# A five-stage tower on one core: the token mixer's parameters computed once, the zero fills spread over the turns, a bias moved between stages, and the second attention's weights in halves with a squared table root

## The chip, the cores and the metric

The kernel runs as one program on one core of a Trainium2 chip. Its time is the device time of one execution in microseconds (us); the median of several executions is compared. One execution was also taken by the hardware profiler, and all rows below come from that one.

## The reference

Sixteen sequences (B = 16) of 257 tokens (T, one class token and 256 others) of width 256 (D) pass through five blocks. All data are float32.

```
h = tok(log_dt, inv_A_real, A_imag, B_ri, x)     # V = exp(log_dA * arange(L)); K = 2 Re(einsum(C*B, V))
h = concat(cls_tok, h)                           # (16, 257, 256)
h = h + retention(layernorm(h))                  # 16 heads, decay mask, group norm, Wout
y = layernorm(h); z = layernorm(y)*g1 + b1
y = y + softmax_attention(z) @ Wp + bp           # causal, 16 heads
y = y + moe(layernorm(y)*g2 + b2)                # 8 experts, top 2
h = h + y
h = h + stablemax_attention(layernorm(h))        # s = 1/(1 - x(1 - x/2(1 - x/3))), x = logits - max
h = h + product_keys(rmsnorm, top 8 of 64 keys)  # gated by retrieved experts
```

The token mixer needs dA = (1 + dtA/2)/(1 - dtA/2) with dt = exp(log_dt), A = -exp(inv_A_real) + i A_imag, and powers of dA. In the second attention all x are at most 0, so a weight is the reciprocal of a cubic in x.

## The kernel before

`tower` calls the stages one after the other; each opens a `Room` with its own buffers and semaphores, and closes with a barrier of all engines. Intermediate tensors go through HBM scratch. Every engine's order is written out by hand, and semaphores set who waits for whom; an engine runs its own list strictly in order. There is no planner.

**token_mixer** (L152) treats 128 pairs of channels in four turns of 32 (PC). For a turn SP loads six pieces of parameters (`load`, L188 to L194). VectorE then runs a chain in `turn`: an exponential by series, the division, and eight squarings E of dA (L258 to L291), 55 operations on tiles of 128 x 32, each of which waits for the one before (`chain.link`); then the powers V and weighted inputs W by doubling (L293 to L315), on tiles of up to 128 x 1024. TensorE multiplies V and W, ScalarE copies out (L225), and SP stores in eight transfers (L203). The engines run the turns in loops (`Fori`); VectorE's and TensorE's have two turns in a pass. V and W have two buffers, and the tile E one.

**retention** (L505) goes over sequences in turns with three overlapping stages: A forms q, k and v of the next sequence, B scores and weighs the present one, C normalises the one before. A turn has 16 steps. SP loads one sequence a turn (L567) and stores in four transfers (L573). ScalarE copies K, V and the results from PSUM. Before its turns ScalarE issues 16 transfers (`FILLS`) of a zero tile of 128 x 4592 floats, 2.3 MB each, into `ys` (L695), rows that the experts' stage uses much later; the stage waits for them at its end. All constants, the decay table of 3.1 MB last, are waited for before the first matmul.

**enter_attention** (L1378) goes over eight groups of 512 tokens and a tail of 16: a projection by TensorE (L1428), h1 = h + projection (L1453), two layer norms in `first`, `second`, `third` on VectorE, transposes (L386), and three stores a group in ScalarE's queue: the transposed x (L1511), hx = h1 + x (L1514) and x (L1515). `first(g+1)` waits until the rows of an earlier group, which use the same buffers, are stored.

**experts** (L1544) starts with a router: for each group of 512 tokens TensorE runs `project` (four tiles of two products with `wp`, L1678, and one product of a row of ones with the bias, L1679), `ranks` of the group before last (per tile a pair of 8-column products, L1702 and L1703), and `gates` (transposes L386, then L1693). VectorE adds the projection to x and to hx (`enter`), picks experts (`choose`), normalises (`leave`) and places (`settle`); POOL scatters rows (L2013). SP's loads of a group wait until two groups before are projected and normalised. 40 tiles of expert work follow.

**attention** (L846) is called twice: causal (softmax), then not causal (stablemax). Its first part projects all sequences and finds the row maxima. The second goes over sequences (a batch) in STEPS = 16 places; the tables `SCORE_AT`, `SUMS_AT` and `VALUE_AT` say at which place an engine does which unit. Not causal, a batch has eight steps v, each for four heads and half of the keys: TensorE forms four 128 x 257 scores in PSUM (L1056), ScalarE squares them (`weigh`, L1193), VectorE makes the cubic (`cubic`, L1311) and frees the scores, and ScalarE takes the reciprocal as exp(-ln) (`log` L1200, `exponential` L1204, each over 128 x 1028). The scores have one set of PSUM banks. For each four heads (two steps) `products` (L1087, L1088), `copy_sums` (L1320), `spread_sums` (L1127), the reciprocal of the sums (L1211, L1218) and `end` (L1327) follow. One table set (`LOG_SET`) is loaded ahead.

## Time and profile before

| what | value |
|---|---|
| median of 3 runs | 4756.81 us (4755.84 to 4758.91) |
| profiled execution | 4754.65 us, its span 4752.8 us |
| granted clock of TensorE, mean | 0.871 |
| token mixer | 0 to 215 us |
| retention | 266 to 622 us |
| entry of attention | 622 to 762 us |
| first attention (causal) | 762 to 1310 us |
| experts, router first (to about 1530) | 1310 to 2294 us |
| second attention, its second part from 2626 | 2294 to 3182 us |
| product keys | 3182 to 4753 us |
| TensorE, VectorE, ScalarE, POOL busy over all | 80%, 52%, 33%, 7% |

Busy times are shares of the span; a stage's start and end are times from the first instruction. PE is TensorE, PEld its weight loads, DVE VectorE, ACT ScalarE, SP the engine that issues most transfers; a q behind an engine's name means its sequencer. Float32 matmuls appear as two instructions each. What stands after `<-` behind an idle time is what ended it. The granted clock is 1.0 at the upper level (2.4 GHz) and 0.5 at the lower (1.2 GHz); a value between them is a mean over a stretch.

### The profile page before, as it was taken

How to read it: one execution, taken by the hardware profiler on the slowest of the kernel's cores; microseconds unless marked ns; L12 is line 12 of the kernel's file. 1: busy time of each engine (PE TensorE's matmuls, PEld its weight loads, DVE VectorE, ACT ScalarE, POOL GpSimd, SP SyncE). 2: the span in 40 equal slices, each digit the busy share in tenths (PEclk: the TensorE clock that was granted, in tenths of full speed). 3: DMA queues.
4: the chain of work that ended last, by engine and by line, in shares of the span. 5: the costliest groups of instructions: out<-in, count | busy, mean ns of one | idle time of the engine just before them, and what ended most of it. 6: DMA issues, size and time to landing. Idle time of an engine off the chain costs nothing. (4 is left out here: it accounts for less than half of the span.)

```text
span 4752.8 us, 94621 instructions
## 1 busy us (share of the span) xinstructions
PE 3820.0 (80%) x38224; PEld 2748.7 (58%) x38224; DVE 2451.1 (52%) x6959; ACT 1567.9 (33%) x2605; POOL 326.3 (7%) x451
## 2 busy tenths in 40 slices
PE   1249946998886899993688777765999999999999
PEld 1236634656554777773344333334877777787776
DVE  8626654542234000003456344427887888888881
ACT  0013312225500323221221788852333333333331
POOL 0011111000024000004100000000000000000000
PEclk8569968999955999996789777866999999999997
DMA  1282142001133545443200000020000000000000
GB/s 33 55 349 83 25 134 78 20 21 32 26 105 104 202 167 186 166 179 120 73 15 15 14 15 18 16 90 28 9 9 15 9 9 15 9 9 15 9 5 5
DMA packets 162688, 295.59 MB, mean 62 GB/s; under 512 B 36688, under 2 KB 138944, under 8 KB 154480
## 3 DMA queue, kind: packets, MB, share of 16 engines
q1 hardware_dynamic: 122720, 199.73, 13.7%
q10 hardware_dynamic: 33296, 73.37, 4.0%
q0 software_dynamic: 6272, 16.85, 1.1%
q8 instruction: 288, 4.72, 0.4%
q14 instruction: 112, 0.92, 0.1%
HBM read 184.17 MB, written 105.20 MB: 61 GB/s over the span
## 5 line engine op out<-in xcount | busy, mean ns | idle before, releaser
L2272 PE MATMUL peer_total<-peer_up,peer_hid 128*128 128x256 f32 (+1 forms) x2112 | 566.0, 395 | 0.0
L2250 PE MATMUL peer_work<-peer_xnT,peer_down 128*128 128x256 f32 (+1 forms) x2176 | 558.4, 380 | 0.0
L2250 PEld LDWEIGHTS peer_work<-peer_xnT,peer_down 128*128 128x128 f32 x2176 | 410.6, 196 | 74.1 <-ACT peer_hid L2303 21.4
L2303 ACT ACTIVATE peer_hid<-peer_work 128x256 f32<-128x256 f32 (+1 forms) x544 | 202.6, 372 | 710.6 <-PE peer_work L2250 710.6
L2272 PEld LDWEIGHTS peer_total<-peer_up,peer_hid 128*128 128x128 f32 (+1 forms) x2112 | 376.5, 187 | 66.8 <-issue 15.3
L2323 ACT ACTIVATE peer_G<-peer_scat 128x512 f32<-128x512 f32 x258 | 272.3, 1056 | 261.5 <-PE peer_scat L2210 261.5
L2421 DVE TENSOR_TENSOR peer_hid<-peer_hid,peer_G 128x256 f32<-128x256 f32 (+1 forms) x544 | 216.3, 407 | 272.1 <-ACT peer_hid L2303 264.1
L1960 DVE TENSOR_TENSOR moe_yb<-moe_bank,moe_w 128x512 f32<-128x512 f32 x40 | 27.7, 692 | 624.1 <-PE moe_bank L1750 624.1
L2210 PEld LDWEIGHTS peer_scat<-peer_one_j,peer_one_i 64*64 64x64 f32 x16448 | 275.3, 138 | 123.2 <-issue 123.0
L1738 PE MATMUL moe_bank<-moe_xgT,moe_w 128*128 128x256 f32 x1280 | 295.2, 384 | 52.0 <-ACT moe_mid L1817 45.7
L2210 PE MATMUL peer_scat<-peer_one_j,peer_one_i 64*64 64x32 f32 x16448 | 302.6, 223 | 36.5 <-DVE peer_one_j L2400 14.6
L1738 PEld LDWEIGHTS moe_bank<-moe_xgT,moe_w 128*128 128x128 f32 x1280 | 230.2, 191 | 105.7 <-ACT moe_mid L1817 61.0
L1750 PE MATMUL moe_bank<-moe_w,moe_mid 128*128 128x256 f32 x1280 | 282.6, 379 | 0.0
L1311 DVE SCALAR_TENSOR_TENSOR stable_U<-stable_U,stable_bank 128x1028 f32<-128x1028 f32 x128 | 156.7, 1224 | 215.6 <-ACT stable_U L1193 215.6
L1750 PEld LDWEIGHTS moe_bank<-moe_w,moe_mid 128*128 128x128 f32 x1280 | 243.2, 190 | 33.1
L1260 DVE TENSOR_REDUCE stable_negmax<-stable_bank 128x2 f32<-128x514 f32 x256 | 168.5, 688 | 125.1 <-PE stable_bank L998 125.1
L1056 PE MATMUL stable_bank<-stable_QT,stable_KT 32*128 32x257 f32 x1024 | 118.5, 531 | 138.9 <-DVEq L1313 138.3
L998 PE MATMUL stable_bank<-stable_KT,stable_QT 32*128 32x257 f32 x1024 | 167.0, 448 | 33.1 <-DVE stable_negmax L1260 32.6
L1817 ACT ACTIVATE moe_mid<-moe_bank,moe_w 128x256 f32<-128x256 f32 x320 | 147.6, 475 | 127.3 <-PE moe_bank L1738 127.3
L1056 PEld LDWEIGHTS stable_bank<-stable_QT,stable_KT 32*128 32x128 f32 x1024 | 54.1, 228 | 201.3 <-issue 201.3
L338 PE MATMUL tok_acc<-tok_V,tok_W 64*64 64x64 f32 x1024 | 37.6, 243 | 165.2 <-DVE tok_prod L316 165.2
L2400 DVE TENSOR_TENSOR peer_one_j<-peer_eq,peer_FT 128x1024 f32<-128x1024 f32 x129 | 158.0, 1225 | 4.4
(361 smaller groups left out, 6320.7 us busy)
## 6 DMA issues: line engine op xcount, KB each, us to landing
moe_w<-in_moe_w SPq DMA_DIRECT2D x40, 2180.0 KB, 8.7
ys<-ret_zeros ACTq DMA_DIRECT2D x16, 2296.0 KB, 52.5
moe_xg<-xs SPq DMA_DIRECT2D x40, 256.0 KB, 8.7
ys<-moe_yb ACTq DMA_DIRECT2D x40, 256.0 KB, 9.0
soft_xT<-xT SPq DMA_DIRECT2D x32, 257.0 KB, 2.8
stable_xT<-xT SPq DMA_DIRECT2D x32, 257.0 KB, 2.8
ret_xT<-xT SPq DMA_DIRECT2D x16, 257.0 KB, 2.8
aT<-ret_cN SPq DMA_DIRECT2D x64, 64.2 KB, 2.1
```

Of the source, the lines that this page charges most:

```text
L998: last = mm(out[:, x, 0:T], QT[rows, b, hg, k * P:k * P + P], KT[rows, b, hg, :], start=True, stop=True)
L1056: last = mm(S[:, j, 0:T], KT[rows, g, hg, k * P:k * P + P], QT[rows, g, hg, :], start=True, stop=True)
L1260: last = v_.tensor_reduce(negmax[:, b % 2, k, at:at + 2], src[:, :, 0:T], AX.X, ALU.max, negate=True)
L1738: last = mm(hid[u % 2], w[:, s, at:at + P], xgT[:, k % 2, c, :], start=c == 0, stop=c == DC - 1)
L1750: last = mm(y[k % 2][:, j, :], mid[:, k % 2, hb, j * P:j * P + P], w[:, s, at:at + D], start=hb == 0, stop=hb == HB - 1)
L2210: last = mm(scat[64 * par:64 * par + 64, half, k * JB:k * JB + JB], one_i[part, s % 2, part_no * SUB // 2 + k, :], one_j[part, s % 2, part ...
L2250: last = mm(work[:, jj % 2, 0:nb], down[:, c, jj, :], xnT[:, g % 3, c, 0:nb], start=c == 0, stop=c == DC - 1)
L2272: last = mm(total[:b_rows, j, :], hid[:, e % NHID, j * P:j * P + b_rows], up[:, e, :], start=e == 0 and j == 0, stop=e == JB - 1, skip_gro ...
L2303: A(hid[:, jj % NHID, 0:nb], work[:, jj % 2, 0:nb], ACT.Gelu).then_inc(gelu_ready, 1)
L2323: A(to, scat[:, 0:halves, 0:SUB // 2 * JB].rearrange("p h (t j) -> p h t j", j=JB), ACT.Copy).then_inc(scat_taken, 1)
L2400: v.tensor_tensor(one_j[:q, s % 2], eq[:q, s % 2], wide(2, NKEYS), ALU.mult).then_inc(one_ready, 1)
L2421: v.tensor_tensor(hid[:, jj % NHID, 0:nb], hid[:, jj % NHID, 0:nb], G[:, g % 2, jj, 0:nb], ALU.mult)\
```

## The change

Five parts:

- token_mixer: parameters of all 128 pairs are loaded at once, and the chain up to the squarings E runs once on tiles of 128 x 128. The turns keep V, W and the products, take slices of E (`mine`), and are written out without loops. The class token is moved behind the parameter loads; B and C, which the turns alone use, have their own semaphore.
- retention: ScalarE issues one fill in each turn that has a stage B, at step 4, instead of 16 ahead of the turns.
- enter_attention and experts: the bias of the projection (`bp`) is added to x by VectorE in the entry stage (`xb`, L1465's neighbour), before hx and the stores; the router's bias products are dropped.
- experts: the ranks of a group are one pair of 32-column products instead of four pairs of 8 columns.
- attention, not causal: scores, square and cubic go in halves of two heads, each with its own signals; the reciprocal is the square of a table function 1/sqrt|x| (`Abs_reciprocal_sqrt`, the set `TABLE_SET[False]`), whose root ScalarE does (`root`) and whose square VectorE does in place (`weigh`), two steps later. Sums and the odd query take both root and square on ScalarE. Sums and values move to other places of the batch. The causal call keeps its operations and places.

```diff
-        tmp = r.sb("tmp", [P, 6, PC])
-        E = r.sb("E", [P, 2, 8, PC])
...
+        tmp = r.sb("tmp", [P, 6, PAIRS])
+        E = r.sb("E", [P, 2, 8, PAIRS])
...
-            def load(t):
-                sp.wait_ge(inputs_free, t + 1)
-                at = bass.ds(t * PC, PC)
-                for h2 in range(2):
-                    half = slice(64 * h2, 64 * h2 + 64)
-                    sp.dma_start(par[half, 0, :], log_dt[h2:h2 + 1, at].broadcast_to([64, PC])).then_inc(loaded, 16)
-                sp.dma_start(par[:, 1, :], inv_A_real[:, at]).then_inc(loaded, 16)
-                sp.dma_start(par[:, 2, :], A_imag[:, at]).then_inc(loaded, 16)
-                sp.dma_start(par[:, 3:5, :], B_ri[:, :, at]).then_inc(loaded, 16)
-                sp.dma_start(c_ri[:, :, :, :], C_ri[:, :, at, :]).then_inc(loaded, 16)
+            for h2 in range(2):
+                half = slice(64 * h2, 64 * h2 + 64)
+                sp.dma_start(par[half, 0, :], log_dt[h2:h2 + 1, :].broadcast_to([64, PAIRS])).then_inc(loaded, 16)
+            sp.dma_start(par[:, 1, :], inv_A_real).then_inc(loaded, 16)
+            sp.dma_start(par[:, 2, :], A_imag).then_inc(loaded, 16)
+            sp.dma_start(par[:, 3:5, :], B_ri).then_inc(weights_in, 16)
+            sp.dma_start(c_ri[:, :, :, :], C_ri).then_inc(weights_in, 16)
...
+            a, b, den, x2, y2, na = (tmp[:, k, :] for k in range(6))
+
+
+            dve.wait_ge(loaded, 64)
+            x, k_, rem, p, dt = par[:, 0, :], tmp[:, 0, :], tmp[:, 1, :], tmp[:, 2, :], ex[:, 0, :]
+            link(v.tensor_scalar(k_, x, 1.0 / LN2, None, ALU.mult))
...
+                mine = slice(t * PC, t * PC + PC)
 
                 dve.wait_ge(products_done, t + 1)
-                link(v.tensor_tensor(E[:, 0, 0, :], x2, den, ALU.mult))
...
+                    e = [E[:, c, k, mine].rearrange("p (a b) -> p a b", b=1).broadcast_to([P, PC, n]) for c in range(2)]
                     q = products(chain, [V[:, c, :, 0:n] for c in range(2)], e[0], e[1], PC * n)
                     v.tensor_tensor(V[:, 0, :, n:2 * n], q[0], q[1], ALU.subtract)
                     link(v.tensor_tensor(V[:, 1, :, n:2 * n], q[2], q[3], ALU.add))
...
+                if t == 0:
+                    dve.wait_ge(weights_in, 32)
+                bb = [par[:, 3 + c, mine].rearrange("p (a b) -> p a b", b=1).broadcast_to([P, PC, B]) for c in range(2)]
...
-                v.memset(prod[:, :, 0:1], 0.0).then_inc(inputs_free, 1)
-                dve.wait_ge(inputs_free, t + 2)
...
-            for k in range(FILLS):
-                act.dma_start(blank[:, k, :], zeros[:, :]).then_inc(filled, 16)
...
+                    if "B" in stages and s == SLOTS:
+                        act.dma_start(blank[:, bass.ds(g, 1), :].rearrange("p o n -> p (o n)"), zeros[:, :]).then_inc(filled, 16)
...
-LOG_SET = "natural_log_exp_and_others"
+TABLE_SET = {True: "natural_log_exp_and_others", False: "abs_reciprocal_sqrt_and_small"}
...
-SUMS_AT = {True: {3: 0, 7: 1, 11: 2, 15: 3}, False: {6: 0, 10: 1, 14: 2, 18: 3}}
+SUMS_AT = {True: {3: 0, 7: 1, 11: 2, 15: 3}, False: {8: 0, 12: 1, 16: 2, 20: 3}}
 SPREAD_LAG, END_LAG = 2, 3
-VALUE_AT = {1: "v0", 4: "v1", 6: "v_odd", 10: "odd_score"}
+VALUE_AT = {True: {1: "v0", 4: "v1", 6: "v_odd", 10: "odd_score"}, False: {5: "v0", 7: "v1", 9: "v_odd", 11: "odd_score"}}
...
+                if not causal:
+                    for x in range(2):
+                        if n:
+                            pe.wait_ge(s_taken, 2 * n + x - 1)
+                            stand()
+                        for j in range(2 * x, 2 * x + 2):
+                            rows = slice(SLOT * j, SLOT * j + SLOT)
+                            last = mm(S[:, j, 0:T], KT[rows, g, hg, k * P:k * P + P], QT[rows, g, hg, :], start=True, stop=True)
+                        last.then_inc(s_ready, 1)
+                    return
...
-                A(w_odd[:, g % 2, :], u_odd[:, :], ACT.Ln, scale=-1.0).then_inc(ln_odd_ready, 1)
+                A(w_odd[:, g % 2, :], u_odd[:, :], ACT.Abs_reciprocal_sqrt).then_inc(ln_odd_ready, 1)
                 act.wait_ge(ln_odd_ready, g + 1)
-                A(w_odd[:, g % 2, :], w_odd[:, g % 2, :], ACT.Exp, scale=-1.0).then_inc(w_odd_ready, 1)
+                A(w_odd[:, g % 2, :], w_odd[:, g % 2, :], ACT.Square).then_inc(w_odd_ready, 1)
...
+            def square(n, x):
+                act.wait_ge(s_ready, 2 * n + x + 1)
+                if n >= 2:
+                    act.wait_ge(ln_ready, n - 1)
+                A(U[:, n % 2, 2 * x:2 * x + 2, :], S[:, 2 * x:2 * x + 2, 0:T], ACT.Square, scale=-SCALE, bias=bend[:, :])\
+                    .then_inc(y_ready, 1)
+
+            def root(n):
+                act.wait_ge(t_ready, 2 * n + 2)
                 if n >= nw:
                     act.wait_ge(av_done, (n - nw) // 2 + 1)
-                A(W[:, n % nw, :, :], U[:, n % 2, :, :], ACT.Ln, scale=-1.0).then_inc(ln_ready, 1)
-
-            def exponential(n):
-                act.wait_ge(ln_ready, n + 1)
-                A(W[:, n % nw, :, :], W[:, n % nw, :, :], ACT.Exp, scale=-1.0).then_inc(w_ready, 1)
+                A(W[:, n % nw, :, :], U[:, n % 2, :, :], ACT.Abs_reciprocal_sqrt).then_inc(ln_ready, 1)
...
-                A(logs[:, n % 2, :], spread_out[:, 0:T], ACT.Ln).then_inc(log_ready, 1)
+                A(logs[:, n % 2, :], spread_out[:, 0:T], ACT.Ln if causal else ACT.Abs_reciprocal_sqrt).then_inc(log_ready, 1)
...
+                            n = g * SU + v
+                            square(n, 0)
+                            square(n, 1)
+                            if n:
+                                root(n - 1)
...
-                u = U[:, n % 2, :, :]
-                dve.wait_ge(y_ready, n + 1)
-                v_.scalar_tensor_tensor(u, u, REST, S[:, :, 0:T], ALU.add, ALU.mult).then_inc(t_ready, 1)
-                dve.wait_ge(t_ready, n + 1)
-                dve.sem_inc(s_taken, 1)
+                for x in range(2):
+                    u = U[:, n % 2, 2 * x:2 * x + 2, :]
+                    dve.wait_ge(y_ready, 2 * n + x + 1)
+                    v_.scalar_tensor_tensor(u, u, REST, S[:, 2 * x:2 * x + 2, 0:T], ALU.add, ALU.mult).then_inc(t_ready, 1)
+                    dve.wait_ge(t_ready, 2 * n + x + 1)
+                    dve.sem_inc(s_taken, 1)
+
+            def weigh(n):
+                w = W[:, n % nw, :, :]
+                dve.wait_ge(ln_ready, n + 1)
+                v_.tensor_tensor(w, w, w, ALU.mult).then_inc(w_ready, 1)
...
+                        n = g * SU + SCORE_AT[causal][s]
                         cubic(g, SCORE_AT[causal][s])
+                        if n >= 2:
+                            weigh(n - 2)
+                    if not causal and g == B and s == 0:
+                        weigh(B * SU - 2)
+                        weigh(B * SU - 1)
...
+            sp.dma_start(next_b[:, :], next_b_in.broadcast_to([P, D])).then_inc(const_in, 16)
...
-                v.tensor_tensor(hx[:rows, q, 0:tiles, :], h1[:rows, q, 0:tiles, :], x[:rows, q, 0:tiles, :], ALU.add)\
+                bias = next_b[:rows, :].rearrange("p (a d) -> p a d", a=1).broadcast_to([rows, tiles, D])
+                chain.link(v.tensor_tensor(xb[:rows, q, 0:tiles, :], x[:rows, q, 0:tiles, :], bias, ALU.add))
+                v.tensor_tensor(hx[:rows, q, 0:tiles, :], h1[:rows, q, 0:tiles, :], xb[:rows, q, 0:tiles, :], ALU.add)\
                     .then_inc(rows_ready, 1)
...
-                act.dma_start(tokens(x_out, t0, tiles, rows), x[:rows, q, 0:tiles, :]).then_inc(rows_stored[q], 16)
+                act.dma_start(tokens(x_out, t0, tiles, rows), xb[:rows, q, 0:tiles, :]).then_inc(rows_stored[q], 16)
...
-                        mm(proj[q][:rows, j, :], aT[:, q, c, j * P:j * P + rows], wp[:, c, :], start=c == 0, stop=False)
-                    last = mm(proj[q][:rows, j, :], ones[0:1, :rows], bp[0:1, :], start=False, stop=True)
+                        last = mm(proj[q][:rows, j, :], aT[:, q, c, j * P:j * P + rows], wp[:, c, :], start=c == 0, stop=c == DC - 1)
...
-                for j in range(tiles):
-                    mm(rank[:rows, j, :], before[:rows, :rows], both[:rows, g % 2, j, :], start=True, stop=False)
-                    last = mm(rank[:rows, j, :], ones[:, :rows], seen[:, g % 2, j, :], start=False, stop=True)
-                last.then_inc(rank_ready, 1)
+                n, flat = tiles * EXPERTS, "p j e -> p (j e)"
+                mm(rank_row[:rows, 0:n], before[:rows, :rows], both[:rows, g % 2, 0:tiles, :].rearrange(flat), start=True, stop=False)
+                mm(rank_row[:rows, 0:n], ones[:, :rows], seen[:, g % 2, 0:tiles, :].rearrange(flat), start=False, stop=True)\
+                    .then_inc(rank_ready, 1)
```

## Rows read from the trace of the kernel before

**Rows 1.** Windows of VectorE, token mixer: length, busy (instructions), granted clock, DMA share, GB/s.
```profile
10.10:22.95 12.85, 10.63 (x55) 1.00 0.00 1
...
22.95:54.95 32.00, 31.08 (x58) 1.00 0.08 19
...
147.70:160.40 12.70, 10.71 (x56) 0.89 0.03 5
```

**Rows 2.** Timeline, token mixer: start us, duration us, engine, line; idle before.
```profile
0.75 0.40 SPq L180 DMA_DIRECT2D tok_cls<-in_cls_tok  x1
...
2.81 1.21 SPq L190 DMA_DIRECT2D tok_par<-in_log_dt  x2
...
10.15 0.18 DVE L258 TENSOR_SCALAR tok_tmp<-tok_par 128x32 f32<-128x32 f32 x1 [9.27 <-DMA tok_c_ri<-in_C_ri]
...
25.29 0.29 DVE L243 TENSOR_TENSOR tok_prod<-tok_V,tok_E 128x128 f32<-128x128 f32 x1
...
102.89 0.18 DVE L258 TENSOR_SCALAR tok_tmp<-tok_par 128x32 f32<-128x32 f32 x1 [3.33 <-issue]
```

**Rows 3.** Timeline, retention's start.
```profile
288.38 1.92 PE L600 MATMUL ret_misc_a<-ret_xT,ret_wk 128*128 128x257 f32 x4
...
314.49 0.39 ACT L716 ACTIVATE ret_KT<-ret_misc_a 128x257 f32<-128x257 f32 x1 [51.06 <-issue]
...
321.94 17.84 SPq L567 DMA_DIRECT2D ret_xT<-xT  x2
...
400.24 0.41 SPq L567 DMA_DIRECT2D ret_xT<-xT  x1
```

**Rows 4.** DMA issues: engine, count, KB each, median us to landing.
```profile
tok_par<-in_A_imag SPq DMA_DIRECT2D x4, 16.0 KB, 1.8
...
ret_decay<-in_decay SPq DMA_DIRECT2D x1, 3088.0 KB, 14.6
...
moe_acc<-hx SPq DMA_DIRECT2D x8, 512.0 KB, 7.1
```

**Rows 5.** Timeline of VectorE, entry of attention.
```profile
689.56 1.22 DVE L1453 TENSOR_TENSOR mid_h<-mid_h,mid_out 128x1024 f32<-128x1024 f32 x1 [4.85 <-DMA x<-mid_x]
...
704.11 1.22 DVE L1453 TENSOR_TENSOR mid_h<-mid_h,mid_out 128x1024 f32<-128x1024 f32 x1 [4.61 <-DMA x<-mid_x]
```

**Rows 6.** Timeline of TensorE, router, and one projection of the entry stage.
```profile
1377.63 2.05 PE L1678 MATMUL moe_bank<-moe_wp,moe_aT 128*128 128x256 f32 x4
...
1379.62 1.22 PE L1679 MATMUL moe_bank<-moe_bp,moe_ones 1*128 1x256 f32 x2
...
1390.22 0.60 PE L1702 MATMUL moe_bank<-moe_both,moe_before 128*128 128x8 f32 x2
...
1393.66 1.95 PE L386 MATMUL moe_bank<-moe_ident,moe_xn 128*128 128x128 f32 x8
...
681.73 4.25 PE L1428 MATMUL mid_out<-mid_wout,mid_cT 128*128 128x256 f32 x16
```

**Rows 7.** Windows, all engines (PE, PEld, DVE, ACT, POOL): six router steps, two batches.
```profile
1354.85:1492.50 137.65, 128.42 (x385) 90.46 (x386) 59.09 (x276) 9.92 (x18) 45.47 (x47) 0.50 0.30 98
...
2700.30:2734.40 34.10, 24.63 (x181) 11.75 (x183) 14.42 (x20) 30.08 (x39) 1.41 (x2) 0.85 0.08 16
...
2734.40:2768.50 34.10, 26.87 (x155) 12.19 (x148) 13.83 (x20) 26.27 (x32) 1.41 (x2) 0.70 0.08 17
```

**Rows 8.** Groups of instructions: count, busy us, mean ns, idle before.
```profile
L1311 DVE SCALAR_TENSOR_TENSOR stable_U<-stable_U,stable_bank 128x1028 f32<-128x1028 f32 x128 | 156.7, 1224 | 215.6 <-ACT stable_U L1193 215.6
...
L1193 ACT ACTIVATE stable_U<-stable_bank,stable_bend 128x1028 f32<-128x1028 f32 x128 | 141.1, 1102 | 12.7 <-PE stable_bank L1056 12.6
...
L1960 DVE TENSOR_TENSOR moe_yb<-moe_bank,moe_w 128x512 f32<-128x512 f32 x40 | 27.7, 692 | 624.1 <-PE moe_bank L1750 624.1
...
L1145 ACT ACT_TABLE_LOAD x2 | 2.6, 1283 | 9.0 <-PEq L74 9.0
```

**Rows 9.** Timeline of VectorE, second attention: a copy behind a cubic.
```profile
2833.20 0.42 DVE L1320 COPY stable_OT<-stable_bank 128x257 f32<-128x257 f32 x1 [0.22 <-DVE stable_U L1311]
```

More of the change, by code:

```diff
@@ L201, in store @@
                         p0 = 64 * h2 + B * a
-                        dst = h_out[:, bass.ds(1 + h2 + t * (2 * PC), PC, 2), L1 * a:L1 * a + L1]
+                        first = 1 + h2 + t * (2 * PC)
+                        dst = h_out[:, first:first + 2 * PC - 1:2, L1 * a:L1 * a + L1]
                         sp.dma_start(dst, res[p0:p0 + B, :, :]).then_inc(stored, 16)
-            load(0)
-            with sp.Fori(0, turns - 1) as t:
-                load(t + 1)
+            sp.dma_start(cls[:, :], cls_tok[0:1, :].broadcast_to([B, D])).then_inc(cls_in, 16)
+            sp.wait_ge(cls_in, 16)
+            sp.dma_start(h_out[:, 0, :], cls[:, :]).then_inc(cls_out, 16)
+            for t in range(turns):
                 store(t)
-            store(turns - 1)
             sp.wait_ge(stored, 16 * 8 * turns + 16)
@@ L225, in copy_out @@
                 nc.scalar.activation(res[:, :, :], acc[:, :, :], ACT.Copy, scale=2.0).then_inc(res_ready, 1)
-            exponential(0)
-            with act.Fori(0, turns - 1) as t:
-                exponential(t + 1)
+            for t in range(turns):
                 copy_out(t)
-            copy_out(turns - 1)
         @block.vector
         def _(dve):
-            nc.vector.memset(prod[:, :, 0:1], 0.0).then_inc(inputs_free, 1)
             v = nc.vector
+            chain = Chain(dve, chained)
+            link = chain.link
             def products(chain, x, er, ei, n):
@@ new lines, in _ @@
+            link(v.scalar_tensor_tensor(rem, k_, -LN2_HI, x, ALU.mult, ALU.add))
+            link(v.scalar_tensor_tensor(rem, k_, -LN2_LO, rem, ALU.mult, ALU.add))
+            link(v.tensor_scalar(p, rem, 1.0 / math.factorial(EXP_TERMS), None, ALU.mult))
+            for n in range(EXP_TERMS - 1, 0, -1):
+                link(v.scalar_tensor_tensor(p, p, 1.0 / math.factorial(n), rem, ALU.add, ALU.mult))
+            link(v.tensor_scalar(two_k[:, :], k_, 127.0, float(1 << 23), ALU.add, ALU.mult))
@@ L317, in turn @@
                 dve.wait_ge(powers_ready, t + 1)
-                chain.done()
-            with dve.Fori(0, turns // 2) as n:
-                turn(2 * n, 0)
-                turn(2 * n + 1, 1)
+            for t in range(turns):
+                turn(t, t % 2)
         @block.tensor
@@ L340, in turn @@
                 last.then_inc(products_done, 1)
-            with pe.Fori(0, turns // 2) as n:
-                turn(2 * n, 0)
-                turn(2 * n + 1, 1)
+            for t in range(turns):
+                turn(t, t % 2)
 def groups(engine, step):
@@ L1217, in invert @@
                     act.wait_ge(ended, n - 1)
-                A(inv[:, n % 2, :], logs[:, n % 2, :], ACT.Exp, scale=-1.0).then_inc(inv_ready, 1)
+                if causal:
+                    A(inv[:, n % 2, :], logs[:, n % 2, :], ACT.Exp, scale=-1.0).then_inc(inv_ready, 1)
+                else:
+                    A(inv[:, n % 2, :], logs[:, n % 2, :], ACT.Square).then_inc(inv_ready, 1)
             odd_score(0)
```

169 lines of the change are left out of this document (70 added, 99 removed).

## The prediction

> **What bounds the kernel now.** The kernel is a row of stages with a barrier behind each, so a stage's gain is the kernel's gain, and each part is read in its own stage. I read the busy time by windows first, to see the stages; then the timeline of one period of each touched stage; then the waits that end last there. The executed time is 4754.65 us (span 4752.8 us, 1.85 us around it); the median of three runs, 4756.81 us, is 2.16 us more, so I work against 4754.65 and add 2.2 at the end. A change within 0.2% (9.5 us) couldn't be told from none.
>
> The token mixer is one VectorE chain. Each of its four turns begins with 55 small dependent operations, 12.85 us in the first and 12.70 us in the last, and goes on with 32 us of long ones; of the 12.85 VectorE is busy 10.63, so a link of width 32 takes 0.19 and a 0.04 us wait [rows 1]. Before it, VectorE stands 9.27 us until the largest parameter load is in, and between the two passes of its loop 3.33 us for "issue" [rows 2].
>
> Retention begins badly: ScalarE idles 51.06 us in "issue" before its first copy, because the sixteen fills of 2.3 MB stand ahead of it in its own order; TensorE has the first K projection done 24 us earlier [rows 3]. The entry of attention is held by a store: VectorE waits 4.85 us of a period of 704.11 - 689.56 = 14.5 us for a landing [rows 5].
>
> The experts' router is TensorE's: in 137.65 us TensorE is busy 128.42, at a granted clock of 0.50, the lower of its two levels (1.2 GHz) [rows 7]. In the second attention, a batch of eight steps takes 34.1 us with ScalarE busy 26 to 30 us, and TensorE at the lower level for part of it (0.70 to 0.85) [rows 7].
>
> **Token mixer.** The 55 links are done once at width 128 instead of four times at width 32. A 128-wide operation took 0.29 us [rows 2]; with the 0.04 wait 55 make 18. Removed: 12.85 + 2 x 12.75 + 12.70 = 51. Gain 33. Bounds: 12.8 if width were free, 23 if a link cost half as much again as that row: 28 to 38. The loop's 3.33 us goes with the loop. At the start four loads are waited for and not six, and the class-token load, its wait and its store no longer stand ahead: the first issue stays at 0.75, the fourth follows 1.9 later (0.6 each, from the pair at 2.81), and A_imag takes 1.8 to land, so VectorE starts at 4.5 and not 10.15, gain 5.6 [rows 2, 4]. The big load, now 2 MB, is needed only after the chain and the first V products, some 35 us on; four times the old one fits there. Later loads disappear from SP's queue, stores stay. VectorE's 32 us per turn, TensorE's products and the last stores stay as they are. The wait for products moves ahead of V only, and the products of two turns back are long done. Sum -42 (-36 to -47).
>
> **Retention.** The fills go into the turns, one per turn. ScalarE can then copy K as soon as TensorE has it: 290.3 (288.38 + 1.92) instead of 314.49, gain 24.2. The constants wait ends with the decay table, 3.1 MB in 14.6 us beside the fills [rows 4]; shared evenly with them it would be half alone, 7 less; I take 5.5 (bounds 0 to 8). Further, the early x loads lie behind the fills: from the issue at 321.94 to that at 400.24 four turns take 78.3 us, where the first of them shows 17.46 (17.84 for two issues less the second's own 0.4) [rows 3]; 78.3 - 69.8 = 8.5 us late, which goes too. On ScalarE one fill per turn costs its issue; it also queues ahead of that turn's four stores and x load. A fill is 2.3 MB, and by the decay row's rate lands in about 11 us, inside a 17.5 us turn. TensorE bounds these turns and ScalarE has slack, so I charge 0.2 us per turn, 3 in all (0 to 12). The last fill starts a turn and a half before the end. Sum -24 - 5.5 - 8.5 + 3 = -35 (-24 to -40).
>
> **Entry of attention.** The added bias addition is a 128x1024 tensor_tensor, 1.22 us as the one in the rows, in each of eight groups. It falls into VectorE's 4.85 us of waiting for a landing; the rows stored in that period were made one period earlier, so their store starts no later [rows 5]. So it is hidden; without the cover it costs 8 x 1.25 + 0.4. One more constant in SP's queue delays the first loads by 0.4 to 1. I take +1 (0 to +11).
>
> **Router.** Each tile's two wp products (2.05) are followed by a one-row bias product; from the first wp product to the first rank product a projection takes 1390.22 - 1377.63 = 12.6 us. Without the bias it is 16 matmuls in a row of the same shape, which the entry stage shows: 4.25 us. The router's own four in 2.05 would be 8.2 for sixteen, so the clock there was at the upper level for a good part [rows 6]. I take 5.5, nearer to the row of the same sequence, since here each projection starts at the lower level; 8.2 is the other bound. Ranks go from four pairs to one: 1393.66 - 1390.22 = 3.4 us to a quarter, 0.9, gain 2.5. The step of 137.65 / 6 = 22.9 becomes 13.3. What comes next: POOL's scatters take 45.47 / 6 = 7.6 us busy in a step and some issue gaps, VectorE has 59.09 / 6 = 9.8 [rows 7], loads land in 7.1 us [rows 4], all inside 13.3. Six steps give 57.6; the first two projections, back to back, 2 x 7.1 = 14; the last two ranks, half hidden by VectorE, 3. Sum -74. With 8.2 per projection: 6 x 6.9 + 9 + 3 = -53. With 4.25, and transposes and gates at the upper level too, a step of 11.4: -91.
>
> **Second attention.** ScalarE loses one of three passes of about 1.1 us per step and splits the square: with 1.1 for a pass and up to 0.35 for the second start, 30.1 - 8 x 1.05 + 8 x 0.35 = 24.5 us per batch at most [rows 7, 8]. VectorE gets that work: eight products of width 1028 (1.22 each, as the cubic of that width) = 9.8; eight split cubics, 2 x 0.69 for 1.22 (0.69 from the 512-wide row), = 1.3 [rows 8]; and after each of 16 halves the 0.22 us hand-over that the copy shows, 3.5 [rows 9]. With 14.4 busy now: 29.0. VectorE becomes the bound: no batch can be under 29.0. Its new wait, for ScalarE's root, is for the root of two steps back, which ScalarE did after the squares of the step before, so it is over when VectorE comes to it. What else is on the path: the weighted products wait for VectorE's square, which comes 1.2 us after the cubic; while TensorE stands there, nothing behind it starts, the next scores included. TensorE's busy time is 24.63 at 0.85 and 26.87 at 0.70 [rows 7], by that slope 22.4 at the upper level and 29.9 at the lower; four waits of 0.9 make 26 and 33.5. So a batch is 29 us at the upper and 33.5 at the lower level; with the share of the lower one as in these two batches (mean 0.78, so 45%) 31. Sixteen batches: 16 x (34.1 - 31) = 50, less 1 for a longer tail: -49. Bounds: -82 (29 throughout), 0 (34.1, TensorE's order binding). In halves the scores of one half run beside the cubic of the other, which takes the old wait of TensorE for VectorE away; that is the reason why VectorE can be kept full.
>
> In this stage one table load stands at the start and none follows, though Square, Identity, Ln and Exp alternate: two loads for two attentions, 1283 ns each [rows 8]. The Trainium skill, page "ScalarE: Activation LUTs", section "Table sets: the hidden batching unit", names relu, copy, identity and abs as filler of every set; Square and the new root are not in that list, and section "What ACT_TABLE_LOAD costs" prices a switch at 2.66 us. If the square needed another set, the rule speaks against the change; that is rival D, worked out from the rows. No row here shows the new set. By the page's price its loads would cost 384 x 2.66 = 1021 us of ScalarE.
>
> **Sum.** -42 - 35 + 1 - 74 - 49 = -199: 4754.65 - 199 + 2.2 = 4558.
>
> **Rivals.** A, the clock takes the second attention's gain: with TensorE at the lower level most of the time, the wait for the squared root replaces the wait for the cubic, batches stay at 34, and the time is 4607. For it: the clock already falls to 0.70 there, and TensorE's gaps remain; against it: less waiting per step means a denser TensorE. B, everything at its better bound: 29 per batch and the router at 11.4: 4558 - 33 - 17 = 4508. For it: the entry stage's rise within one projection. C, the fills do not leave the path: if each fill issued in a turn holds ScalarE as long as the early ones did (51.06 / 16 = 3.2 us), retention gains nothing, 4593. Against: those filled the queue, one per turn doesn't. D, slower: the table of the new set lacks Square. Then each step switches to the root and back, and sums twice per group: up to 24 loads per batch at 1.28 = 30.8 us; ScalarE's batch is 24.5 + 30.8 = 55.3, and 16 x 21.2 = 339 us are lost against 150 won elsewhere: 4946. It ends slower than before from 15 loads per batch on. Against: the old set held Square beside two transcendentals.
>
> **Chances.** Forecast (4530 to 4585) 0.52, A 0.20, B 0.16, C 0.08, D 0.04. The parts don't depend on one another, so a shortfall in one doesn't turn the sign: faster 0.95, same 0.01, slower 0.04. The range reaches from B to a little beyond A: 4502 to 4630.
>
> **What would show it.** Token mixer: 55 links once, its stage over near 173 of the span (215 now). Retention: ScalarE's first K copy within 1 us of its projection, turns of 17.5 from the first. Router: no 1-row matmuls, step 12 to 14.5, granted clock above 0.50. Second attention: one table load, VectorE busy over 75%, batches of 29 to 33. The forecast is wrong if batches stay at 34, if the router's step stays above 15, or if any stage not touched moves.

## The result, and the profile after

The changed kernel takes 4567.23 us, the median of four runs (4555.41 to 4583.38), against 4757.86 of the kernel before on the same chip (4755.84 to 4763.22). The ratio is 0.960, its 95% interval 0.957 to 0.963. The forecast was 4558. The profiled execution took 4574.35 us, 180.3 less than the one before; its stages, from the first instruction to the last (transfers left out):

| stage | before | after | start to start, change | forecast |
|---|---|---|---|---|
| token mixer | 203.9 | 157.7 | -42.5 (with its start) | -42 |
| entry of retention (untouched) | 48.1 | 48.6 | +0.5 | 0 |
| retention | 351.1 | 317.5 | -33.6 | -35 |
| entry of attention | 135.4 | 138.1 | +2.9 | +1 |
| first attention (untouched) | 543.6 | 545.6 | +2.0 | 0 |
| experts with the router | 980.0 | 900.9 | -79.1 | -74 |
| second attention | 882.5 | 849.6 | -32.8 | -49 |
| last stage (untouched) | 1567.9 | 1570.2 | +2.3 | 0 |

The token mixer's first two times begin at different points, a short memset at 0.82 us before and the first link at 4.81 after, so its change is read from the start of the next stage.

Token mixer: the window of VectorE from its first instruction to the end of the chain (length, busy and instructions, granted clock, DMA share, GB/s). It answers to the first line of [rows 1]: 18.15 us once in place of four times 12.7 or more. It begins at 4.81 instead of 10.15 [rows 2].
```profile
4.81:22.96 18.15, 16.29 (x55) 1.00 0.30 113
```

Retention: the timeline around the first K copy. ScalarE follows the projection of 242.33 at once, with no "issue" in front of it as in [rows 3].
```profile
242.33 1.63 PE L588 MATMUL ret_misc_a<-ret_xT,ret_wk 128*128 128x257 f32 x4
...
244.06 0.39 ACT L704 ACTIVATE ret_KT<-ret_misc_a 128x257 f32<-128x257 f32 x1 [22.63 <-PE ret_misc_a L588]
```
Its DMA issues (count, KB each, median us to landing): a fill lands in 9.9 us, where the page of before has 52.5, and the decay table in 10.3 instead of 14.6 [rows 4].
```profile
ys<-ret_zeros ACTq DMA_DIRECT2D x16, 2296.0 KB, 9.9
...
ret_decay<-in_decay SPq DMA_DIRECT2D x1, 3088.0 KB, 10.3
```

Entry of attention, VectorE: the new addition stands at L1478, and the wait for the landing, 4.85 in [rows 5], is 3.60: the cover paid for it. The period stays at 617.19 - 602.64 = 14.55 us.
```profile
602.64 1.22 DVE L1465 TENSOR_TENSOR mid_h<-mid_h,mid_out 128x1024 f32<-128x1024 f32 x1 [3.60 <-DMA x<-mid_xb]
611.14 1.23 DVE L1478 TENSOR_TENSOR mid_xb<-mid_x,mid_next_b 128x1024 f32<-128x1024 f32 x1
...
617.19 1.22 DVE L1465 TENSOR_TENSOR mid_h<-mid_h,mid_out 128x1024 f32<-128x1024 f32 x1 [3.57 <-DMA x<-mid_xb]
```

Router, timeline of TensorE, answering to [rows 6]: sixteen products in 5.27 us, one pair of rank products instead of four, and ahead of the next projection a new wait, for a load.
```profile
1281.42 5.27 PE L1692 MATMUL moe_bank<-moe_wp,moe_aT 128*128 128x256 f32 x16 [0.70 <-DMA moe_acc<-hx]
1286.53 0.30 PE L1715 MATMUL moe_bank<-moe_both,moe_before 128*128 128x32 f32 x2
1286.67 0.39 PE L1716 MATMUL moe_bank<-moe_seen,moe_ones 128*128 128x32 f32 x2
...
1296.60 0.80 PE L1692 MATMUL moe_bank<-moe_wp,moe_aT 128*128 128x256 f32 x1 [5.14 <-DMA moe_acc<-hx]
```

Windows over all engines (PE, PEld, DVE, ACT, POOL busy, then granted clock, DMA share, GB/s), answering to [rows 7]: six router steps; the second part of the second attention, from its first square to its end; and two neighbouring stretches of it, one at each level of the clock.
```profile
1270.21:1344.61 74.40, 54.24 (x265) 46.21 (x265) 56.78 (x269) 9.92 (x18) 44.42 (x45) 0.77 0.54 179
2478.83:2994.77 515.94, 453.23 (x2596) 218.63 (x2596) 396.93 (x572) 342.79 (x558) 21.17 (x29) 0.73 0.08 15
2680.64:2694.30 13.66, 11.49 (x88) 5.48 (x86) 12.25 (x19) 11.30 (x21) 1.42 (x2) 1.00 0.21 40
2694.30:2711.37 17.07, 16.37 (x76) 7.77 (x76) 12.45 (x18) 9.24 (x14) 0.00 (x0) 0.50 0.00 0
```
The same part of before:
```profile
2628.08:3177.34 549.26, 406.44 (x2595) 183.19 (x2593) 229.46 (x316) 451.85 (x558) 20.98 (x29) 0.78 0.07 14
```
The router's step is 74.4 / 6 = 12.4 us. In the second attention ScalarE's load went to VectorE (229 to 397 us busy), and the part lost 33.3 us. In these two stretches VectorE is busy 12.25 of 13.66 us at the upper level, TensorE 16.37 of 17.07 at the lower: a different engine is nearly full in each. I counted the 127 steps by the granted clock at their middle: 68 at the upper level with 3.32 us on average, 59 at the lower with 4.67; before, 78 with 3.94 and 49 with 4.71. The lower level holds 54% of the time instead of 44%. These means are no price of the clock, because they hold different kinds of steps: after the change v = 0, 1 and 2 fall at the lower level in 45 of 48 cases, v = 4, 5 and 6 at the upper level in 45 of 48. By kind, v = 5 fell from 6.5 us to 3.5, and v = 2 rose from 4.1 to 7.2 and v = 0 from 4.1 to 5.1, since products, sums and values were moved to other places.

The long step v = 2 (7.19 us) in TensorE's timeline, at the lower level: products, odd products and a value unit, 5.2 us, all ahead of the next scores.
```profile
2673.37 1.94 PE L1081 MATMUL stable_bank<-stable_W,stable_V 128*32 128x257 f32 x16
2675.24 1.22 PE L1082 MATMUL stable_bank<-stable_w_odd,stable_V_odd 16*128 16x257 f32 x2
2676.39 2.07 PE L1111 MATMUL stable_bank<-stable_wv,stable_xT 128*128 128x256 f32 x4
2678.39 1.24 PE L1046 MATMUL stable_bank<-stable_QT,stable_KT 32*128 32x257 f32 x8
```
Groups of the second attention, as in [rows 8]: VectorE's halves of 0.69 us, its square, and still two table loads for two attentions.
```profile
L1309 DVE SCALAR_TENSOR_TENSOR stable_U<-stable_U,stable_bank 128x514 f32<-128x514 f32 x256 | 176.5, 690 | 64.4 <-ACT stable_U L1188 44.8
...
L1316 DVE TENSOR_TENSOR stable_W<-stable_W 128x1028 f32<-128x1028 f32 x128 | 157.2, 1229 | 18.8 <-DVE stable_U L1309 0.5
...
L1139 ACT ACT_TABLE_LOAD x2 | 2.6, 1283 | 9.3 <-PEq L74 9.3
```
VectorE's two halves in its timeline, 1.53 us together:
```profile
2687.51 1.53 DVE L1309 SCALAR_TENSOR_TENSOR stable_U<-stable_U,stable_bank 128x514 f32<-128x514 f32 x2
```

### The profile page after: what moved, and what is told of

It reads as the page before. It is cut to its first block and busy times, and to the rows that moved or that the text cites. A ratio compares the mean times of both kernels' runs of the same rounds, so it can differ in the third digit from the quotient of the medians.

```text
span 4572.5 us, 94477 instructions
## 1 busy us (share of the span) xinstructions
PE 3759.8 (82%) x38062; PEld 2721.0 (60%) x38062; DVE 2602.4 (57%) x7054; ACT 1458.2 (32%) x2602; POOL 326.6 (7%) x451
## 5 line engine op out<-in xcount | busy, mean ns | idle before, releaser
L1188 ACT ACTIVATE stable_U<-stable_bank,stable_bend 128x514 f32<-128x514 f32 x256 | 164.9, 681 | 156.4 <-PE stable_bank L1046 152.6
L1309 DVE SCALAR_TENSOR_TENSOR stable_U<-stable_U,stable_bank 128x514 f32<-128x514 f32 x256 | 176.5, 690 | 64.4 <-ACT stable_U L1188 44.8
L1046 PE MATMUL stable_bank<-stable_QT,stable_KT 32*128 32x257 f32 x1024 | 182.2, 550 | 19.6 <-DVEq L1311 17.5
L986 PE MATMUL stable_bank<-stable_KT,stable_QT 32*128 32x257 f32 x1024 | 167.6, 449 | 32.8 <-DVE stable_negmax L1257 32.4
L1316 DVE TENSOR_TENSOR stable_W<-stable_W 128x1028 f32<-128x1028 f32 x128 | 157.2, 1229 | 18.8 <-DVE stable_U L1309 0.5
```

What stands on the lines that cost most here:

```text
L986: last = mm(out[:, x, 0:T], QT[rows, b, hg, k * P:k * P + P], KT[rows, b, hg, :], start=True, stop=True)
L1046: last = mm(S[:, j, 0:T], KT[rows, g, hg, k * P:k * P + P], QT[rows, g, hg, :], start=True, stop=True)
L1309: v_.scalar_tensor_tensor(u, u, REST, S[:, 2 * x:2 * x + 2, 0:T], ALU.add, ALU.mult).then_inc(t_ready, 1)
```

## Experiments

Theory: the gain is a sum over stages, and in the second attention it is cut by TensorE at its lower level. Rivals: VectorE or the root sets the batch and the clock is a bystander; or the halves are the gain. Barriers keep the stages apart, so one kernel can carry an edit in several. "Part" is the second attention from its first square to its end, "batch" eight steps of it (the mean of the first fifteen batches), "lower share" the share of the time from the first square to the last at the lower level; single executions unless a range is given. The same part was profiled in three executions, the changed kernel twice and once in the kernel before (below): 515.9, 520.4 and 515.3 us. So a difference of some 5 us between two kernels says nothing.

**Unused products of 128 rows, and of 32.** Behind the scores of v = 6, 7, 0 and 1, into PSUM columns that nobody reads:
```
+ free = O[((s - 2) // 4) % 2]
+ for x in range(1):     # at s in (1, 3, 13, 15); 128 -> 32 in the second kernel
+     mm(free[:, 258:512], spread[0:128, :], KT[0:128, g, x % HG, 0:254], start=True, stop=True)
```
Where the expectations, here and below, speak of eight products a batch, two in each place, the kernels have one in each place: four a batch, 60 in all, which the trace records as two instructions each (2716 instead of 2596).

> The changed kernel with eight unused products per batch of the second attention (two 128-row products of 254 columns in each of four steps that have only 32-row scores: behind v = 6, 7, 0 and 1). In the changed kernel a step takes 3.32 us while the granted clock is at the upper level and 4.67 at the lower, and the lower one holds 54% of the time. Theory (TensorE at the lower level sets the step there, and the clock falls where TensorE has little but 32-row scores): the lower share falls under 0.35, batches from 31.5 to 27.5 to 29.5, second part of the stage from 516 to 445 to 480 us, whole kernel 4500 to 4540. Rival (VectorE or the root sets the step, the clock is a bystander): the share may move, the batch stays at 31.5 or more, the part at 516 or more. Second rival (the clock doesn't answer to it): share 0.54, and eight products of about 0.5 us make the batch 2 to 4 us longer.

> The same eight unused products per batch in the same places, with 32 rows in place of 128. Theory (what TensorE does in those steps decides its clock, and 32-row products don't raise it): the lower share stays near 0.54 or grows, the batch is 31.5 to 35 us. Rival (any product that fills the gap does it): share and batch as with 128 rows.

Windows of the part, 128 rows and then 32:
```profile
2474.83:2954.49 479.66, 409.46 (x2716) 198.82 (x2716) 392.50 (x572) 338.41 (x558) 21.10 (x29) 0.91 0.08 16
```
```profile
2490.55:3021.38 530.83, 482.50 (x2716) 253.19 (x2716) 396.86 (x572) 342.45 (x558) 21.14 (x29) 0.72 0.07 15
```
The same 60 additional products made the part 36 us shorter with 128 rows (lower share 0.16, batch 29.1) and 15 us longer with 32 (share 0.56, batch 32.5); the kernels took 4535.38 and 4600.11 us, all as expected. VectorE's work is the same in both. So the clock is no bystander, and between these two kernels it went with the rows of the products.

With 128 rows five batches ran at 1.00 throughout; one of them, and one of the changed kernel for comparison:
```profile
2652.53:2680.63 28.10, 24.02 (x175) 11.70 (x172) 24.52 (x37) 21.13 (x37) 1.42 (x2) 1.00 0.10 20
```
```profile
2664.61:2696.66 32.05, 29.18 (x166) 14.30 (x166) 25.07 (x37) 21.51 (x35) 1.42 (x2) 0.71 0.09 18
```

**Three parts undone, one per stage.**
```
router:     + mm(proj, ones[0:1, :rows], bp[0:1, :], start=False, stop=True)   # entry as before
retention:  + for k in range(FILLS): act.dma_start(blank[:, k, :], zeros)      # ahead of the turns
attention:  - square(n, 0); square(n, 1)      + square(n)     # cubic and scores in full width too
```


> The changed kernel with one part undone in each of three stages, which barriers keep apart: the one-row bias products back in the router (and the entry stage as before), the sixteen fills ahead of retention's turns, the second attention in full width with the new root and VectorE's square. Expected: router's projection back from 5.5 to about 12.6 us, its step from 12.4 to 19 to 21, clock at 0.50; retention from 317.5 to about 351; entry of attention from 138 to 135.4. Second attention, theory (halves keep VectorE and TensorE beside each other): scores, square and cubic follow one another again, batches of 33 to 35. Rival (the pass taken from ScalarE is the gain, halves do nothing): 31 to 32.

Windows of five router steps and of the part, and the router's timeline:
```profile
1313.47:1415.45 101.98, 94.29 (x262) 62.68 (x262) 49.15 (x230) 8.26 (x15) 36.52 (x37) 0.50 0.36 119
2566.88:3092.49 525.61, 417.95 (x2596) 195.83 (x2596) 378.09 (x444) 323.77 (x430) 21.14 (x29) 0.72 0.07 15
```
```profile
1313.47 2.05 PE L1682 MATMUL moe_bank<-moe_wp,moe_aT 128*128 128x256 f32 x4
1315.45 1.22 PE L1683 MATMUL moe_bank<-moe_bp,moe_ones 1*128 1x256 f32 x2
```
Projection 12.59, step 20.4 us, all at 0.50; the experts stage is 962.2. Retention is 350.4 us, the entry 134.9: as expected. The second attention lost only 9.7 us (batch 32.3), or 5 against the longest execution with halves: between the two expectations, nearer to the rival that the halves do little.

**Three other edits.**
```
router:     mm(proj, ident[:, :rows], bp[:, :], ...)     # 128 rows instead of 1, same sum; entry as before
retention:  8 fills ahead; then one half fill per turn
attention:  - v_.tensor_tensor(w, w, w, ALU.mult)   + A(W, W, ACT.Square)   # halves and root kept
```


> The changed kernel with three other edits in three stages. Router: the same bias products with 128 rows (identity by a bias row on every partition) in place of one row. Theory (one-row products hold the clock down): projection 6.5 to 8 us, step 12.5 to 14.5, clock well above 0.50; rival (their time alone counted): projection 12.6, step 19 to 21, clock 0.50. Retention: eight fills ahead, the rest in half fills, one per turn. Theory (a full DMA queue held ScalarE): ScalarE's first K copy within 1 us of its projection, stage 318 to 325; rival (the fills' share of the DMA engines): copy still 10 us or more late, stage 330 or more. Second attention: halves and new root, the square on ScalarE as a third pass. Theory (ScalarE was the bound before and is so again, 21 + 8 x 1.06 = 30 us busy per batch): 32 to 35; rival (VectorE's new square is the present bound): under 31.

Windows, router's timeline, and DMA issues (count, KB each, us to landing):
```profile
1282.64:1350.00 67.36, 58.08 (x261) 50.93 (x262) 48.57 (x230) 8.25 (x15) 35.61 (x36) 0.75 0.55 180
2493.85:3012.89 519.04, 468.69 (x2596) 224.62 (x2596) 249.38 (x444) 455.22 (x686) 21.08 (x29) 0.70 0.07 15
```
```profile
1286.47 0.59 PE L1696 MATMUL moe_bank<-moe_bp,moe_ident 128*128 128x256 f32 x2
1286.91 1.03 PE L1695 MATMUL moe_bank<-moe_wp,moe_aT 128*128 128x256 f32 x4
```
```profile
ret_decay<-in_decay SPq DMA_DIRECT2D x1, 3088.0 KB, 14.8
ys<-ret_zeros ACTq DMA_DIRECT2D x8, 2296.0 KB, 33.0
```
Router: the same number of products as with one-row bias, at 0.75 instead of 0.50; projection 6.9 to 7.5, step 67.36 / 5 = 13.5 us. Of the 10.5 us that the change took off a step, the ranks are 2.5 (22.9 to 20.4), the clock that came with the one-row products 6.9 (20.4 to 13.5), and the rest 1.1 (13.5 to 12.4): the bias products' own time, less the wait for the rows' load, which grew from 0.3 us a step to 1.8. Retention: the K copy follows its projection at once (249.57, projection from 247.62), yet the stage is 328.9 us, 11.4 more than with fills in turns and longer than expected: the shared DMA engines cost that. The decay table lands 4.5 us later, and the next two loads of x take 15.2 and 16.1 us instead of 2.6. The other 21.5 (350.4 - 328.9) are for the most part ScalarE held by its queue: from the first projection to the first product with the decay table 38.1 us pass with sixteen fills ahead, 17.8 with eight. Second attention: batch 32.0, at the low end of what was expected; but the part, 519.0, lies within the three executions with VectorE's square (515.3 to 520.4), so at this clock that square brought nothing that can be seen.

So at this clock neither undoing the halves nor undoing VectorE's square gives back much of the 33.3 us. Both kernels keep the later places of the root, the sums and the values: in the kernel before, ScalarE took the logarithm in the same step as the cubic that it waits for, and now it takes the root one step later. What these places alone bring, no run separates.

**The second attention's part alone, in the kernel before.**

> The kernel before with nothing but the second attention's part of the change. Theory (stages are kept apart by barriers, gains add up): stage 849 to 852 us from start to end against 882 before and 850 with all parts, all other stages as before within 3 us, whole kernel 4720 to 4728. Rival (a stage's clock depends on what ran before it): the stage differs by over 10 us from the 850.

848.8 us, 0.2 below the expected range, and 4717.76 in all, 2.2 below; all other stages within 1.4 us of before. The gains add up over stages.

**Value products moved, without and with unused products.**
```
- False: {5: "v0", 7: "v1", 9: "v_odd", 11: "odd_score"}
+ False: {7: "v0", 11: "v1", 14: "v_odd", 15: "odd_score"}     # the odd query's weights at s = 1
```


> The changed kernel with the value products of the second attention moved behind the scores of the odd steps (v0 behind v = 3, v1 behind 5, the odd ones behind 7), where no weighted products stand; no unused products. Theory (at either level the next scores wait on TensorE behind products and a value unit in one step): the long step v = 2 falls from 7.19 to 5 us, the even steps to 3.3 at the upper level, batch 29 to 31. Rival (VectorE sets the step, TensorE's order is no matter): batch 31.5, the time only moves between steps. What the clock does with the new order is open; were it to stay low for longer, the batch could be 32 or more.

> The same move, and four unused 128-row products per batch, behind the scores of v = 1 and v = 7. Theory (both the order and the clock count): lower share under 0.25, batch 27 to 28.5, second part of the stage 435 to 460 us, whole kernel 4490 to 4520. Rival (with the clock up, VectorE is the bound whatever TensorE's order): 29, as with the eight unused products alone.

Both missed: batches of 34.0 and 32.0, 4609.0 and 4574.69 us. The steps v = 0 and v = 2 did fall, from 5.12 to 2.86 and from 7.19 to 4.98; but v = 7 rose to 9.57, because the odd score now stood right behind the odd values and waited for VectorE's copy of them (2.80 us) and then took 3.58 us (1.90 at the upper level in the changed kernel), the next scores behind it:
```profile
2709.90 3.58 PE L1104 MATMUL stable_bank<-stable_QT,stable_K_odd 128*16 128x257 f32 x8 [2.80 <-DVE stable_v_odd L1301]
2713.41 1.24 PE L1046 MATMUL stable_bank<-stable_QT,stable_KT 32*128 32x257 f32 x8
```
A wait that I had added myself stands in these two; the mended move below, with the same number of unused products, takes it out.

**The changed kernel again, the unused products timed, and the move mended** (odd values one step earlier; one, two and one unused products at s = 1, 3, 15):
```
+ False: {7: "v0", 11: "v1", 13: "v_odd", 15: "odd_score"}
```


> The changed kernel once more, for its spread: 4555 to 4584 us, ratio to before 0.957 to 0.963. Theory (the second attention's time follows the share of the lower clock, which differs from run to run): times fall with the mean granted clock of the run; rival: no relation.

> The changed kernel with the eight unused 128-row products, timed: 4525 to 4545 us, below every run of the changed kernel by over 10 us, if the clock in the second attention is what its lower batches came from; 4555 or more in some runs if the first look was a lucky phase.

> As the move with four unused products, but the odd rows' value product behind v = 6 and their score behind v = 7, one step apart, so that TensorE doesn't stand behind the copy between them (2.80 us of waiting and a step of 9.57 in the run with the move alone). Theory (that wait was all that the move lost): no step above 4.5 us, batch 25 to 27.5, second part of the stage 405 to 445, whole kernel 4470 to 4510. Rival (the move costs the clock what it saves in order): batch 29 or more.

| kernel | median of 4 (range) | ratio to before (95%) |
|---|---|---|
| changed, again | 4568.56 (4560.38 to 4579.94) | 0.961 (0.959 to 0.964) |
| four unused products a batch | 4548.48 (4532.55 to 4560.91) | 0.956 (0.953 to 0.959) |
| values moved, four unused products a batch | 4519.47 (4494.81 to 4522.56) | 0.949 (0.945 to 0.952) |

Window of the part in the third kernel:
```profile
2486.41:2943.89 457.48, 378.47 (x2716) 202.19 (x2716) 389.31 (x572) 344.97 (x558) 21.11 (x29) 0.94 0.08 17
```
The third beats both kernels: 49 us less than the changed one. Its batch is 27.8 us, lower share 0.09, no step of a batch above 4.3 on average. It missed what was expected in all three times: the batch (27.5 at most), the part (12 us above the range) and the median of the kernel (9 us above). As it has no more unused products than the second, only other places for them and the values, what it gains on the second comes from the order. The second is 20 us better than the changed kernel in the median, but it missed too: its slowest run is above three of the eight of the changed kernel. Its profiled part, 478.1 us, agrees with the 479.7 of the first execution, so the gain in this part came twice; where its four runs differ isn't known. The changed kernel's eight runs order by their mean clock: 0.889 with 4555 us, 0.887 and 0.888 with 4560 to 4561, 0.883 with 4583. But the theory put this down to the second attention, and that isn't borne out: in the second profile of the changed kernel the whole was 14 us faster although this stage took 859.5 us instead of 849.6. The difference between the two lies in the last stage, which the change doesn't touch: its last 55 us ran at 0.53 in the first profile of the changed kernel and at 1.00 in the second, where the stage took 1546.6 us instead of 1570.2.
```profile
4517.00:4572.00 55.00, 52.27 (x162) 27.81 (x160) 4.98 (x27) 4.64 (x26) 0.00 (x0) 0.53 0.00 1
```
```profile
4503.00:4558.00 55.00, 52.30 (x280) 36.59 (x278) 10.38 (x43) 9.20 (x41) 0.00 (x0) 1.00 0.02 6
```

**With the clock mostly up: full width, and the square on ScalarE.** The four unused products a batch of the first experiment, together with full width as in the kernel with three parts undone, and with the square on ScalarE.

> The eight unused 128-row products as in the first such run, and the second attention in full width instead of halves. At the clock of the changed kernel full width cost only 0.75 us a batch. Theory (at the lower level TensorE sets the step and hides what the halves bring; at the upper level they show): with the clock mostly up, full width is 1.5 to 3 us a batch slower than halves with the same products (29.1): 30.6 to 32. Rival (halves bring next to nothing): 29 to 30.

> The eight unused 128-row products, halves and the new root, but the square on ScalarE as a third pass. At the changed kernel's clock this cost 0.46 us a batch (32.0 against 31.5). Theory (what VectorE's square brings shows only at the upper level: ScalarE was 98% busy there, 3.67 us a step): with the clock mostly up, batches of 30 to 31.5 against 29.1, even with ScalarE over 95% busy at the upper level. Rival (TensorE's order sets the step at either level, the third pass is hidden): 28.5 to 29.5.

```profile
2479.16:2962.89 483.73, 374.57 (x2716) 179.77 (x2716) 377.04 (x444) 324.16 (x430) 22.19 (x29) 0.92 0.08 16
```
```profile
2481.98:2994.26 512.28, 478.78 (x2716) 230.21 (x2716) 248.74 (x444) 455.47 (x686) 21.08 (x29) 0.80 0.08 15
```
Full width takes 483.7 us against 479.7 with halves, batch 29.5 against 29.1, at about the same clock, a difference within the spread of one kernel: the rival was right, halves bring next to nothing. The third ScalarE pass makes it 512.3 (batch 31.4); but its clock was lower too (share 0.40), so how much of the 33 us is the pass and how much the clock stays open. At the upper level ScalarE was busy 98% and a step took 3.63 us against 3.44, means over unlike steps, so that isn't a clean price of the pass either.

## Why the prediction was right, and where it was not

- **Token mixer** (-42.5 for -42): the chain at 18.15 for 18, the start at 4.81 for 4.5. Right in both.
- **Retention** (-33.6 for -35): three terms were off and cancelled. From the stage's start to the first projection 4.05 us went (19.99 to 15.94), for the 5.5 of the decay table; from there to the first product with the decay table 26.9 (38.9 to 12.0), for 24.2; and all the rest 2.6, for the 8.5 of late x loads. Turns already ran at 17.8 us before, so most of the loads' lateness was hidden. The 3 us charged for fills in the turns were not there: 17.8 again. The mechanism named for the K copy was shown; the share of the DMA engines counted beside it: eight fills alone, with ScalarE free, cost 11.4 us.
- **Entry of attention** (+2.9 for +1): the addition is hidden in the steady period, as said. Not counted: the first projection comes 1.8 us later, behind one more constant, and the first addition, with nothing to hide it, cost 1.6.
- **Router** (-79.1 for -74): projection 5.1 to 6.5 for 5.5, step 12.4 for 13.3. That the clock would be at the upper level for a good part was the right reason for choosing 5.5; the run with 128-row bias products shows that the clock is most of this gain, 6.9 of 10.5 us a step. Two things are missing in the sum and nearly cancel: transposes and gates ran at the upper level too (1.07 us for 1.95 and 1.95 for 3.58, 2.5 a step, counted only in the better bound), and the load of the rows comes late (10.9 us of waiting in six steps, 1.8 a step), which the prediction had held to be inside the step.
- **Second attention** (-32.8 for -49, and only -23.0 in the second profile): the step that failed is the sum for the batch. 31.5 us for 31 came out near, by errors that partly cancel. The share of the lower level was taken as it had been, 45%; it became 54%, and with the forecast's own 29.0 and 33.5 that alone gives 31.4. But these two were off as well. At the upper level "no batch can be under 29.0" is refuted: with the same work on VectorE, and four more products on TensorE, a batch at 1.00 takes 28.1; VectorE is busy for 24.5 of it, where the forecast had 25.5 (29.0 less the hand-overs). Nor does a hand-over of 0.22 follow each half: two halves in a row take 1.53 us, 2 x 0.69 and 0.15. No batch ran at the lower level throughout; from 32.05 at 0.71 and 28.1 at 1.00 one there would take some 35 (an estimate, by the shares of time at each level), for 33.5. From the first square to the last 37.2 us were gained for the 50 of the forecast, and the tail grew by 3.9 instead of 1. The mechanism given for a full VectorE, that halves take TensorE's old wait away, isn't borne out: full width costs 5 to 10 us at the changed kernel's clock and 4 with the clock mostly up. What the runs show in its place is TensorE's clock and order: 36 us by the 128-row products, and with the values moved another 21 to 22. Which part of the change brought the 33 us themselves stays open. Rival A's batches of 34 did not come, but its premise, that the clock takes a part of the gain, held.
- **The table set** (rival D): one load of 1283 ns at the stage's start, none after it. The rule of the Trainium skill that was weighed there (page "ScalarE: Activation LUTs", section "Table sets: the hidden batching unit") would have acted only with Square outside the set of the new root; the trace shows that it is inside. B did not happen; C did not either, fills in turns land in 9.9 us.
- **Untouched stages** moved by 0.5, 2.0 and 2.3 us. That was named as a sign of error; the second profile shows that the last stage alone moves by 23.6 us between two executions of one kernel, so the sign was drawn too narrowly.

The sum, -180.3 in the profiled pair and -190.6 between the medians for a forecast of -199, was right because four of the five parts of the sum came out within 5 us. The fifth, the second attention, fell short by 16 us, of which the router's extra 5 hide a part; that much is luck.

## What to carry to other kernels

Read the granted clock by stretch beside each engine's busy time, and compare the same kind of step, or whole periods, at each level: a mean over all steps at one level mixes kinds. Where TensorE is nearly full at the lower level, relieving another engine may bring little there. Undo each part of a change alone: here two parts that were expected to carry a stage's gain gave back little. A small product on TensorE may cost more by the clock that comes with it than by its own time; replace it or widen it and look at the clock, before counting its microseconds. When a unit is moved in an order written out by hand, look at what it waits for and what stands behind it in its new place.

## What the runs showed of the hardware that was not expected

- TensorE was granted 0.50 in five router steps while it was busy for 94.29 of 101.98 us; with the bias products at 128 rows instead of one, 0.75 at 58.08 of 67.36.
- More work on TensorE shortened a part of a stage: 60 unused 128-row products, 515.9 to 479.7 us; with 32 rows 530.8.
- Sixteen fills of 2.3 MB ahead on ScalarE's queue held it (most of 21.5 us of the stage); eight did not, its copy came at once, and still cost 11.4 us by the landing of other loads (decay table 14.8 us instead of 10.3, the next loads of x 15.2 and 16.1 instead of 2.6).
